# A third buffer, in SBUF, for the decay factors of a selective scan

## The reference, cut to what matters

```python
dA = jnp.exp(delta[..., None] * A)
dBu = (delta * u)[..., None] * B_ssm[:, :, None, :]
def step(h, inp):
    dA_i, dBu_i, c_i = inp
    h = dA_i * h + dBu_i
    y = jnp.einsum('bds,bs->bd', h, c_i)
    return (h, y)
```

## Time and profile before

| | |
|---|---|
| median of 3 runs | 3182.5 us (3182.36 to 3185.03) |
| the profiled execution | 3180.75 us, span from first to last instruction 3179.0 us |
| scans of the 16 sequences | 146 to 2515 us of the span |
| experts | from about 2580 us |
| VectorE, 400 to 1500 us | 1047.56 us busy |
| TensorE, 400 to 1500 us | 990.71 us busy |
| GpSimd, 400 to 1500 us | 872.33 us busy |
| ScalarE, 400 to 1500 us | 823.10 us busy |

### The profile page before, as it was taken

One profiled execution on the slowest core, in us unless ns is written; L12 is line 12 of the kernel. 1 busy time (PEld: TensorE's weight loads), 2 busy tenths in 40 slices (PEclk: granted clock), 3 DMA queues, 4 the chain that ended last, 5 costly groups with the idle time before them and its releaser, 6 DMA issues. The chain is left out here.

```text
span 3179.0 us, 47169 instructions
## 1 busy us (share of the span) xinstructions
PE 2799.8 (88%) x13205; PEld 1852.2 (58%) x13206; DVE 2488.6 (78%) x4112; ACT 2060.8 (65%) x3797; POOL 2156.5 (68%) x2202
## 2 busy tenths in 40 slices
PE   4777989898989898989889898989897789999998
PEld 2445555655555565656565555555655547777776
DVE  3599999999999999999999999999998632222222
ACT  3677777787867777777777777778675324444443
POOL 1378787787878687869687878788787514444443
PEclk8898999999999899999999999999898889999999
DMA  2043434343434343433434343434347323334433
GB/s 79 21 103 74 101 83 100 78 108 82 103 75 99 81 108 76 100 84 94 94 90 95 88 97 83 100 82 107 75 104 187 98 55 62 63 63 63 63 61 52
DMA packets 147356, 272.54 MB, mean 86 GB/s; under 512 B 19873, under 2 KB 78306, under 8 KB 147170
## 3 DMA queue, kind: packets, MB, share of 16 engines
q0 software_dynamic: 57840, 152.07, 26.8%
q1 hardware_dynamic: 79106, 109.65, 10.8%
q10 hardware_dynamic: 10224, 8.57, 0.8%
HBM read 107.16 MB, written 45.63 MB: 48 GB/s over the span
## 5 line engine op out<-in xcount | busy, mean ns | idle before, releaser
L914 POOL TENSOR_TENSOR dbu<-du,bbc 128x512 f32<-128x512 f32 x1024 | 1338.8, 1387 | 146.9 <-DVE h L1505 138.5
L1505 DVE TENSOR_TENSOR_SCAN h<-bank,dbu 128x512 f32<-128x512 f32 x1024 | 1220.4, 1210 | 48.1 <-ACT bank L1134 45.5
L1134 ACT ACTIVATE bank<-region,amat 128x512 f32<-128x512 f32 x1024 | 702.5, 689 | 102.2 <-DVE h L1505 97.0
L697 PE MATMUL bank<-ident,h 128*128 128x128 f32 x4096 | 625.2, 288 | 118.7 <-DVE acc L1495 51.5
L697 PEld LDWEIGHTS bank<-ident,h 128*128 128x128 f32 x4096 | 494.4, 148 | 402.1 <-DVE acc L1495 134.8
L1118 ACT ACTIVATE hTc<-bank,cT 128x512 f32<-128x512 f32 x448 | 306.5, 684 | 235.2 <-PE bank L697 130.2
L1675 POOL DMA_INDIRECT out<-ye,ids x135 | 212.2, 1572 | 345.2 <-DMA out<-ye,ids 312.5
L1495 DVE SCALAR_TENSOR_TENSOR acc<-bank,cT,acc 128x512 f32<-128x512 f32 x576 | 416.4, 730 | 23.3 <-PE bank L697 21.8
L651 PE MATMUL bank<-x4T,w_su 128*128 128x512 f32 (+1 forms) x768 | 375.5, 610 | 9.9 <-ACT region L961 8.5
L900 POOL DMA_DIRECT2D acc<-hTc x224 | 203.1, 907 | 262.4 <-ACT hTc L1118 250.4
L1711 DVE SCALAR_TENSOR_TENSOR gg<-gt,bank 128x352 f32<-128x352 f32 x135 | 70.3, 520 | 383.6 <-ACT gt L1645 383.6
(11 more groups left out here) (221 smaller groups left out, 4261.4 us busy)
## 6 DMA issues: line engine op xcount, KB each, us to landing
acc<-hTc POOLq DMA_DIRECT2D x224, 512.0 KB
bbc<-b_scratch SPq DMA_DIRECT2D x256, 256.0 KB
xe<-slots_in SPq DMA_DIRECT2D x135, 129.0 KB
region<-in_x SPq DMA_DIRECT2D x16, 512.0 KB, 3.8
out<-x ACTq DMA_DIRECT2D x16, 512.0 KB, 3.3
region<-in_e_gu SPq DMA_DIRECT2D x8, 704.0 KB
out<-ye,ids POOLq DMA_INDIRECT x135
slots_in<-dbu SPq DMA_DIRECT2D x16, 129.0 KB, 3.1
```

The source lines that it names most:

```text
L697: last = tr(scan[f"hT{s}.{t}"][:, m * P:(m + 1) * P], h[:, s % 2, m, t * P:(t + 1) * P], ident[:, :])
L914: g.tensor_tensor(dbu[:, n % 4, :], du[:, m, :], bbc[:, (b * NS + s) % NROW, :], ALU.mult).then_inc(S("dbu_ready"), 1)
L1134: f(db(n)[:, :], delta[:, 1 - par, m, :], ACT.Exp, scale=amat[:, m, s:s + 1]).then_inc(S("da_ready"), 1)
L1505: v.tensor_tensor_scan(h[:, s % 2, m, :], db(n)[:, :], dbu[:, n % 4, :], 0.0, ALU.mult, ALU.add)\
```

## The change

Factors go round three buffers instead of two: bank 6, bank 7 and a new SBUF tile `da` of 128x512 fp32. Which one is chosen by the running number of the unit over all sequences, modulo 3. The Exp of unit n waits for scan n-3 instead of n-2. To make room in SBUF, the four integer tables are laid over the start of `region`, and `amat` takes the place of `alog`.

```diff
-        eidi, rowi, runi = psb("eidi", [1, SLOTS_T], i32), psb("rowi", [1, SLOTS_T], i32), psb("runi", [1, E], i32)
-        fencei = psb("fencei", [1, SLOTS_T], i32)
+        eidi, rowi, fencei, runi = (region[0:1, k * SLOTS_T:k * SLOTS_T + n].bitcast(i32) for k, n in enumerate((SLOTS_T, SLOTS_T, SLOTS_T, E)))
...
-        alog, amat = sb("alog", [P, MC, NS]), sb("amat", [P, MC, NS])
+        alog = amat = sb("amat", [P, MC, NS])
...
+        da = sb("da", [P, T])
...
-        def db(n):
-            return banks[6 + n % 2]
+        def decay(b, n):
+            return (banks[6], banks[7], da)[(b * UNITS + n) % 3]
...
-                    before(act, "scan_done", b, n - 1)
-                    f(db(n)[:, :], delta[:, 1 - par, m, :], ACT.Exp, scale=amat[:, m, s:s + 1]).then_inc(S("da_ready"), 1)
+                    before(act, "scan_done", b, n - 2)
+                    f(decay(b, n)[:, :], delta[:, 1 - par, m, :], ACT.Exp, scale=amat[:, m, s:s + 1]).then_inc(S("da_ready"), 1)
...
-                    v.tensor_tensor_scan(h[:, s % 2, m, :], db(n)[:, :], dbu[:, n % 4, :], 0.0, ALU.mult, ALU.add)\
+                    v.tensor_tensor_scan(h[:, s % 2, m, :], decay(b, n)[:, :], dbu[:, n % 4, :], 0.0, ALU.mult, ALU.add)\
```

## The result

The changed kernel takes 3402.8 us (median of 4 runs, 3401.57 to 3404.91) against 3182.4 us before (4 runs, 3181.77 to 3185.03). The ratio is 1.069, 95% interval 1.067 to 1.071. The kernel got slower, and by the lock that was forecast; but the loss is 220 us where 109 were forecast, and the time lies 3 us over the top of the range, 3400. The sum had a scan wait for one operation of GpSimd, and the scans waited for one to four.

What follows compares the result with a forecast made beforehand. VectorE, 95% busy in the scan loops, was taken as the bound. The terms +133 + 3 + 15 - 12 - 30 = +109 us on 3182.5 us gave 3291 us, range 3185 to 3400 us.

Steps and rivals of the forecast that it cites:

- The bound: In the scan loops VectorE is busy 95%, so a microsecond added to its stream is nearly a microsecond of the kernel.
- The lock: A VectorE operation with two SBUF inputs can't run while GpSimd reads SBUF; read from one long L1387 comparison.
- Its size: Scans reading da wait for half of a GpSimd operation with chance 0.62: 341 x 0.39 = 133 us.
- (c): Rival: GpSimd goes first at every border between operations, so scans wait longer: 134 us more, 3425 us; chance 0.08.
- GpSimd's lateness: GpSimd, held back by da scans, delays the DMA into acc, hTc copies and next Exp: 15 us, bounds 0 and 133.
- The form: A two-input operation on SBUF alone takes 9 ns more than with a PSUM operand: 3 us on 341 scans.
- Gain and absorption: Third buffer removes 12 us of VectorE's waits for factors; VectorE's idle time in the loop absorbs 30 us.
- ten stalls: VectorE's factor waits at unit 20, in 10 of 16 batches: cost 20 us, stay or shrink by VectorE's delay.
- ScalarE: ScalarE's waits for scans fall from 97 to under 30 us; writing the Exp to SBUF costs 0.

Runs made afterwards that it cites:

- the own wait: The changed kernel, but GpSimd waits after each dbu multiplication until it is done, so the next is never issued behind a running one: 3355.4 us, ratio 1.056.
- the shorter lead: The changed kernel, but GpSimd's dbu of unit n waits for scan n-2 instead of n-4: 3645.2 us, ratio 1.146.
- the iota: GpSimd fills dbu with zeros by an iota instead of multiplying: 3225.9 us in the changed kernel, 3184.9 us in the kernel before.
- eight quiet units: The changed kernel with da only for eight units per sequence where GpSimd is mostly quiet, the others taking the two banks in turn: 3192.4 us, ratio 1.003.
- the kernel without the lead: The changed kernel with its three buffers, but the Exp of unit n waits for scan n-2 as before: 3416.6 us, ratio 1.074.

## Why the prediction was wrong, by its own steps

**The bound.** Right. VectorE took up 36 us of the added 255 in its idle time; the rest came through.

**The lock.** Right as a mechanism, though read off one long case among 16 of L1387, with its release 0.12 us before the end of GpSimd's record. In the changed kernel waiting scans begin 0.11 to 0.13 us before that end (186 of 188), and a GpSimd operation that only writes doesn't hold them.

**Its size, the term that failed.** The sum had 341 x 0.39 = 133 us: a chance of 0.62 to meet an operation, times half of its length, 0.63 us. Measured: 188 of 341 meet one, 0.55, and each waits 1.41 us; 341 x 0.777 = 265 us. The chance was a little too high, the wait 2.2 times too low. The step that failed is the silent one, that a scan waits for the operation it meets and no more. Split by the trace, the 188 wait 148 us for the first operation, near the 133 of the sum, and 117 us for further ones, which the sum put at nothing. This was rival (c), which got 0.08 where the trace before showed nothing for either side. Its price was 134 us more, near the 132 by which the term was short; in part that is luck, since (c) had 106 scans wait for one more operation, and in fact 83 scans waited for 104 more between them, up to three each. The prediction named the back-to-back multiplications and the four deep ring, and both bear on it: GpSimd can have three `dbu` and whatever lies between them ready while one scan waits, since all that would stop it is that scan. With the own wait the old reading holds far better: 163 us, 212 x 0.77.

**GpSimd's lateness.** Charged 15 us. VectorE's waits for `dbu` went from 1.9 to 16.3 us, 14.4 more, so the size fits. The path that the text gave for it, through the DMA into `acc` and the `hTc` copy, doesn't show: ScalarE's waits for that DMA fell from 104.8 to 36.8 us (it shows only with the shorter lead). The number was in part luck.

**The form.** Charged 3 us for two SBUF inputs. With the iota the undisturbed `da` scans lie within 5 ns of the others, so about nothing. The saving of 65 ns that the Trainium skill's page "VectorE: DVE Perf Modes" gives in its table of the TRN2 errata doesn't show there either.

**Gain and absorption.** -12 and -30, together 42. VectorE's idle time shrank by 36.4 us net of the 14.4 of new waits for `dbu`, so by 51 us without them. The sum is 9 us short of that, the shares aren't settled: taking the lead away costs 14 us in the changed kernel, but the lead brought nothing with eight quiet units or with the iota. Of the ten stalls of 1.9 to 1.98 us at unit 20 one is left, of 1.89 us, and VectorE's waits for factors are 9 us in all; the text let them "stay or shrink by VectorE's delay", and the kernel without the lead shows that it was the delay.

**ScalarE.** Its waits for scans fell to 48 us, not under 30. The Exp into `da` takes 717 ns against 686 into a bank, 31 ns more, hidden in its idle time.

With 265 in the place of 133 the sum of the prediction gives 3182.5 + 241 = 3423 us, 20 us over the measured time. The top of the range came from giving (c) next to no chance, though its time had been worked out as 3425 us.

## What to carry to other kernels

Before a VectorE input moves from PSUM to SBUF, look whether its other input is in SBUF and whether GpSimd reads SBUF at the same time; the move may turn a free scan into a queue behind another engine. When a trace shows one case of a lock, price not the rest of one operation but the rest of the run that the other engine has ready, and ask what ends that run: here it was the waiting scan itself, by way of a ring of four. And before adding a buffer, ask whether the producer's place in its own list of instructions lets it use the lead: in none of these runs did the third one make VectorE faster than the kernel before.

## What the runs showed of the hardware

GpSimd keeps the port between operations when the next one is already issued: 83 of 341 scans stood behind two to four reading operations and waited up to 4.5 us, some of them across the issue of a DMA. With a wait between the operations, 212 of 212 waiting scans got in after one; behind a DMA issue the multiplication that follows holds a scan up to 0.54 us before its record begins. The Trainium skill, page "SBUF — State Buffer", section "SBUF: two separate sides", has the holder keep the pair "for the whole instruction"; these runs show it kept for longer. A GpSimd iota of 647 ns held no scan (63 started while one ran and kept their time); a copy of 745 ns with one SBUF input did (52 of 58). And a held-back GpSimd multiplication takes up to 2.29 us in the changed kernel, where the longest before took 1.66, so both sides can lose.
